# Own keys for the first two units, merged maxima tiles in the first chunk, and a new order of work

## The reference

```
h  = LN(x)
p  = h @ W_state.T + b_state ;  g = sigmoid(h @ W_gate.T + b_gate)
s_t = tanh(p_t + s_{t-1})                 # 1024 steps, one after the other
x1 = x + LN(g * s)
u  = LN(x1)
q, k, v = heads of rms(u) @ wq.T, wk.T, wv.T   (16 heads of 16; q, k are normed)
u += (softmax(causal(q k' / 4)) v) @ wo.T      (first 64 columns left as they are)
xf = rms(u) ; top 2 of 4 experts by softmax(xf @ gate_w.T)
u += sum of weights * expert(xf)               (all four experts are computed)
out = x1 + LN(u)
```

## Time and profile before

| | |
|---|---|
| median of 3 runs | 1585.27 us (1581.87 to 1589.87) |
| profiled execution | 1589.69 us |
| its span, first to last instruction | 1588.0 us |
| busy PE / DVE / ACT / POOL | 1403.0 / 1098.6 / 952.3 / 319.2 us |
| granted TensorE clock, mean | 0.933 |

### The profile page before, as it was taken

How to read it: one execution, slowest core, us unless ns; L and a number is a source line. 1 busy time by engine, 2 the same in 40 slices (tenths; PEclk the granted TensorE clock), 3 DMA queues, 4 the chain that set the end, 5 groups by cost and what they waited for, 6 DMA issues and landing times. The chain is left out here.

```text
span 1588.0 us, 33694 instructions
## 1 busy us (share of the span) xinstructions
PE 1403.0 (88%) x12320; PEld 1108.8 (70%) x12320; DVE 1098.6 (69%) x2916; ACT 952.3 (60%) x2092; POOL 319.2 (20%) x1146
## 2 busy tenths in 40 slices
PE   6915679999979799998998999999999999999997
PEld 3404567889867568688885577876686667857697
DVE  7776577553886975858888569786788777773342
ACT  2535465675556777775555673538546676468941
POOL 3343333223333323232332110001000010000000
PEclk9956578999998999899998899999999999999999
DMA  5585336754675545546656455665656657556343
GB/s 170 147 285 151 112 103 195 217 152 142 181 227 184 184 138 169 184 125 201 204 177 191 150 161 168 223 193 153 205 178 207 202 170 216 180 189 202 123 144 112
DMA packets 244276, 278.54 MB, mean 175 GB/s; under 512 B 37136, under 2 KB 167696, under 8 KB 243856
## 3 DMA queue, kind: packets, MB, share of 16 engines
q1 hardware_dynamic: 244112, 276.39, 56.6%
HBM read 234.18 MB, written 43.45 MB: 175 GB/s over the span
## 5 line engine op out<-in xcount | busy, mean ns | idle before, releaser
L1702 POOL TENSOR_TENSOR AD<-PX 128x8 f32<-128x8 f32 x1023 | 250.4, 245 | 553.3 <-ACT PX L928 537.3
L928 ACT ACTIVATE PX<-AD 128x8 f32<-128x8 f32 x1023 | 219.3, 214 | 232.0 <-POOL AD L1702 229.8
L996 ACT ACTIVATE work<-PS 128x1024 f32<-128x1024 f32 (+1 forms) x312 | 288.7, 960 | 79.5 <-PE PS L1042 77.8
L1501 DVE TENSOR_REDUCE mx<-PS 128x2 f32<-128x1024 f32 (+3 forms) x256 | 256.7, 1020 | 81.0 <-PE PS L1042 79.9
L1042 PE MATMUL PS<-work,vlx 128*32 128x256 f32 (+2 forms) x2816 | 240.6, 381 | 18.3 <-ACT work L996 7.5
L1042 PE MATMUL PS<-EP,u_e_l 128*128 128x256 f32 x1024 | 199.4, 289 | 6.9 <-DVE EP L1367 4.5
L1709 POOL TENSOR_SCALAR_AFFINE_SELECT work<-work 128x512 f32<-128x512 f32 x96 | 63.8, 674 | 638.1 <-ACT work L996 637.9
L1042 PE MATMUL PS<-WB,work 128*128 128x192 f32 x1024 | 181.2, 330 | 3.6 <-ACT work L1021 1.3
L1021 ACT ACTIVATE work<-PS 128x512 f32<-128x512 f32 x176 | 104.2, 596 | 132.7 <-PE PS L1042 131.2
L1042 PE MATMUL PS<-EP,WB 128*128 128x256 f32 x640 | 182.3, 285 | 0.0
L1042 PE MATMUL PS<-KT,QT 64*128 64x512 f32 (+3 forms) x768 | 151.9, 434 | 27.8 <-DVE mx L1501 12.9
(11 more groups left out here) (170 smaller groups left out, 2345.8 us busy)
## 6 DMA issues: line engine op xcount, KB each, us to landing
KT<-ktd SPq DMA_DIRECT2D x112, 512.0 KB, 4.8
WB<-wlo_e_l SPq DMA_DIRECT2D x160, 256.0 KB, 3.0
WB<-wlo_e_up SPq DMA_DIRECT2D x64, 256.0 KB, 3.0
ktd<-KTs SPq DMA_DIRECT2D x128, 128.0 KB, 2.2
WB<-wlo_e_w SPq DMA_DIRECT2D x64, 256.0 KB, 2.9
WB<-wdn_e_down SPq DMA_DIRECT2D x64, 192.0 KB, 2.7
KT<-ktd SPq DMA_DIRECT2D x48, 256.0 KB, 3.5
KT<-ktd SPq DMA_DIRECT2D x32, 384.0 KB, 4.1
```

Source lines behind the costliest of these rows:

```text
L928: eng.activation(cur, AD[n % 2], ACT.Tanh).then_inc(of(*key), 1)
L996: eng.activation(pt[:, :, :, q0:L], two("sc", *a).rearrange("p a (l q) -> p a l q", l=2)[:, :, :, q0:L], ACT.Exp).then_inc(of(*key), 1)
L1501: eng.tensor_reduce(o, two("mxm", *a)[:, :, 0:w], AX, ALU.max, negate=True).then_inc(of(*key), 1)
L1702: eng.tensor_tensor(AD[n % 2], PX[c % 2][:, :, :, t], PX[(n - 1) // L % 2][:, :, :, (n - 1) % L], ALU.add).then_inc(of(*key), 1)
```

## The change

Three edits.

1. Units 0 and 1 (`u < 2`) no longer use `KTs`. Their key tiles s = 0, 1 are copied to the two tiles of one `EP` pair (`own_keys`), and `mxm` and `sc` read them there. `ktm` and `kts` are not issued for these units. `kst` stays, with its source changed. The pair is held until the unit's last score (`sc`, group 3) and both stores are done.
2. In chunk 0 (`u < B`, four units) a maxima tile takes both planes of a group: 8 tiles in a unit instead of 16, each with twice the columns, and `mxr` reduces four rows of maxima at once.
3. New numbers in `STAY`, `START` and `AT`, thus another order on each engine.

```diff
-STAY = {"pe": 18.5, "act": 7.0}
+STAY = {"pe": 24.2, "act": 5.7}
-START = (114.6, 163.8, 192.7, 269.5, 332.7, 421.8, 507.9, 597.9, 743.8, ...)
+START = (101.2, 162.6, 177.3, 239.6, 336.5, 416.5, 521.4, 595.3, 735.9, ...)
 (all 27 rows of AT are new too)

 def tiles_of(u):
+            if u < B:
+                tiles.append((j, s, planes, 0, n))
+            else:
+                tiles += [(j, s, (pl,), k0, min(512, n - k0)) for pl in planes for k0 in range(0, n, 512)]

 arrange:
-  kt: take={"P2": (("kc", u, s),), "KTs": (("kst", u, s),)}
+  kt: take={"P2": (("kc", u, s),), **({"KTs": (("kst", u, s),)} if u >= 2 else
+        {"EP": (("sc", u, 3, 0), ("kst", u, 0), ("kst", u, 1))} if s == 0 else {})}
+            if u >= 2:
                 add("sp", ("ktm", u, j), ...)
-            for h in range((nkb + 3) // 4):
+            for h in range((nkb + 3) // 4) if u >= 2 else ():
                 add("sp", ("kts", u, g, h), ...)

+        def own_keys(u, s):
+            return EP[place[("kt", u, 0), "EP"]][s].rearrange("p k t -> p (k t)").rearrange("p (a k) -> p a k", a=8)

 mxm:
+                    if u < 2:
+                        kt = own_keys(u, s)[:, 2 * g:2 * g + 2, :]
+                        pe.wait_ge(*latest([("kc", u, 0), ("kc", u, 1)]))
+                    for x, pl in enumerate(pls):
+                        for par in range(2):
+                            ins = mm(ps[:, par, w * x:w * x + w], ..., x == 0, True, True)

 mxr:
+                    if len(pls) == 2:
+                        o = mx[:, s, :].rearrange("p (a h) -> p a h", a=2)[:, :, h:h + 2]
+                        x = two("mxm", *a)[:, :, 0:2 * w].rearrange("p a (l k) -> p a l k", l=2)
```

More of the change, by code:

```diff
@@ new lines @@
+STAY = {"pe": 24.2, "act": 5.7}
+START = (101.2, 162.6, 177.3, 239.6, 336.5, 416.5, 521.4, 595.3, 735.9, 806.3, 936.0, 1005.2, 1113.3, 1190.3, 1307.3, 1390.6)
+AT = {"piece": (-133.2, 84.2, 12.4, 109.4),
+      "post": (105.4, 80.1, -59.9, -28.2),
+      "prep": (-63.5, -85.9, -72.0, -5.3),
+      "value": (-196.8, 20.6, -143.0, -140.6),
+      "key": (-99.0, -64.8, 33.5, -55.6),
+      "query": (-40.6, -49.2, -91.2, -34.5),
+      "max": (-51.3, -43.8, -48.4, -39.2),
+      "maxima": (15.6, 0.5, 10.4, 44.6),
+      "bound": (71.1, -14.0, 109.5, 111.6),
+      "score": (37.1, 42.8, 43.2, 49.8),
+      "scores": (20.9, 11.4, 14.7, 16.6),
+      "av": (23.2, -22.9, 0.9, 17.7),
+      "merge": (22.7, -32.9, -7.9, 4.8),
+      "out": (-224.8, -29.1, -112.8, -84.9),
+      "gate": (-85.6, -244.9, -66.5, 50.2),
+      "l1": (7.3, 231.4, 238.0, 215.2),
+      "e0up": (189.4, 158.2, 57.5, 322.4),
+      "l2": (210.2, 275.6, 218.4, 193.1),
+      "e0dn": (371.7, 297.1, 375.7, -49.8),
+      "e1": (295.9, 250.0, 345.8, 230.4),
+      "l3": (220.9, 302.9, 201.9, 305.6),
+      "e3dn": (165.8, 332.2, 223.1, 268.9),
+      "e1dn": (272.2, 315.1, 325.6, 359.6),
+      "l4": (209.0, 255.5, 79.8, 276.9),
+      "e3up": (321.2, 310.5, 300.0, 298.5),
+      "e3out": (190.8, 294.9, 331.7, 465.0),
+      "fin": (230.3, 202.3, 202.0, 472.2)}
@@ L353, in arrange @@
             add("dve", ("kh", u, s), 2.33, d, ("qrs", u), ("cqk", 0), ("consts",), take={"QKP": (("kt", u, s),)})
[L354 removed]
+            add("pe", ("kt", u, s), 0.645, d, ("kh", u, s), mode="128", lat=DRAIN,
+                take={"P2": (("kc", u, s),), **({"KTs": (("kst", u, s),)} if u >= 2 else {"EP": (("sc", u, 3, 0), ("kst", u, 0), ("kst", u, 1))} if s == 0 else {})})
             add("act", ("kc", u, s), act(1024), d, ("kt", u, s))
@@ L366, in arrange @@
             dj = d + at["maxima"] * j / len(jobs)
-            add("sp", ("ktm", u, j), 0.35, dj - 5, *keys, *([("ktm", *prior["ktm"])] if "ktm" in prior else []), lat=4.5, take={"KT": (("mxm", u, ends[j]),)})
-            prior["ktm"] = (u, j)
-            for i, (j_, s, pl, k0, w) in enumerate(tiles):
+            if u >= 2:
+                add("sp", ("ktm", u, j), 0.35, dj - 5, *keys, *([("ktm", *prior["ktm"])] if "ktm" in prior else []), lat=4.5, take={"KT": (("mxm", u, ends[j]),)})
+                prior["ktm"] = (u, j)
+            for i, (j_, s, pls, k0, w) in enumerate(tiles):
                 if j_ != j:
@@ L1130, in _ @@
                     u, i = a
-                    j, s, pl, k0, w = tiles_of(u)[i]
+                    j, s, pls, k0, w = tiles_of(u)[i]
                     g, planes = jobs_of(u)[j]
-                    kt, n = KT[place[("ktm", u, j), "KT"]], 128 * key_blocks(u)
-                    kt = keys_of(kt[:, 512 * s:], 2, n) if u < B else keys_of(kt, len(planes), n)
+                    n = 128 * key_blocks(u)
+                    if u < 2:
+                        kt = own_keys(u, s)[:, 2 * g:2 * g + 2, :]
+                        pe.wait_ge(*latest([("kc", u, 0), ("kc", u, 1)]))
+                    else:
+                        kt = KT[place[("ktm", u, j), "KT"]]
+                        kt = keys_of(kt[:, 512 * s:], 2, n) if u < B else keys_of(kt, len(planes), n)
+                        pe.wait_ge(*done("ktm", u, j))
@@ L1144, in _ @@
-                    if diag < w:
+                    for x, pl in enumerate(pls):
+                        for par in range(2):
+                            rows = slice(64 * par, 64 * par + 64)
+                            ins = mm(ps[:, par, w * x:w * x + w], qt[rows, 2 * g + pl, 128 * s:128 * s + 128],
+                                     kt[rows, pl - planes[0], k0:k0 + w], x == 0, True, True)
+                    for x in range(len(pls)) if diag < w else ():
                         for i in range(2):
```

42 lines of the change are left out of this document (22 added, 20 removed).

## The result

The changed kernel takes 1593.51 us (median of 18 runs, 1588.54 to 1598.75), the kernel before 1585.48 (18 runs, 1576.40 to 1591.12). The ratio is 1.0052, 95% interval 1.0037 to 1.0068: slower by 8.2 us (5.9 to 10.8). Forecast were 1575 us and "faster", with an outer range of 1558 to 1594 and a chance of 0.16 for slower. So the time lies just inside the range, and the direction is wrong. So the two traces differ by 1.1 us where the medians differ by 8.0. They can show what moved; the price has to come from timed runs.

The account below looks back on a forecast made before the run. TensorE bounds it from 280 us, with holes before 280 and after 402. Experts 19 us earlier: 7 + 3, plus 1 + 2, is 13; less 3 given back, 10 off 1585.27 makes 1575 us (1567 to 1583; outer 1558 to 1594).

Parts of the forecast that it names:

- Edits, first part: Units 0 and 1, own keys: maxima start 4.7, their pass 6, scores 8; unit 0's experts 19 us earlier, near 211.
- named marks of success: Unit 0's maxima before 150, output projection before 200, first expert before 215; TensorE work over 40 from 160 to 230.
- Edits, second part: Merged maxima tiles, units 0 to 3: 4.9 us less VectorE work, 1 us added to the gain.
- What the earlier experts are worth: Before 280: 19 us at 0.80 instead of 0.44 give 7 us, unit 1's experts 3; 10 together.
- what is given back at the gate: After 402: step 511 stays, so experts done before are missing; 0 to 10 us given back, taken as 3.
- The new order: Newly searched order on all engines: taken as 2 us gained, with -10 to +12 as ends.
- The third rival: Recurrence late beside earlier experts: gate 6 us later, 10 missed, 4 for order, against 10 won; 1595, chance 0.17.
- the sum's own gain: Before 280: 10 us from earlier experts, 1 from merged maxima and 2 from the order, 13 us.
- The first rival: Work pulled out of 402 to 557 is missed there one for one: 3 us less, 1582, chance 0.22.
- the named signs of failure: First expert after 225, unit 0's second layer waiting, gate after 408, or 402 to 600 losing what the first stretch won.
- The rule of the Trainium skill: VectorE and GpSimd share a port lock: reductions from PSUM cost the recurrence nothing, experts' subtractions hold it up; no term changed.

Follow-up runs that it names:

- k3: Kernel before, every engine's order kept, with both edits (own keys and merged maxima tiles): 0.9996 (0.9968 to 1.0023) of before, median 1587.62 us.
- k9: Changed kernel with 45 recurrence steps between 204 and 508 left out, order otherwise kept, output not the reference's: 1.0053 of the kernel before.
- k13: Both edits; order of the kernel before up to 640 us, the changed kernel's behind it: 1.0027 of before, 1591.21 us.
- k14: Both edits; the changed kernel's order up to 640 us, that of the kernel before behind it: 1.0132 of before, 1608.25 us.
- the kernels of the table: Both edits in all; orders of the kernel before and the changed kernel, whole or crossed at 640 or 150 us: 0.9996 to 1.0132 of before.
- k11: Both edits with due times from a new search that replays orders with disturbed durations: 1.0065 of before, median 1598.05 us.
- k12: Both edits with due times from a second result of that disturbed-duration search, from another start: 1.0081 of before, median 1598.28 us.
- k5: Changed kernel with six exponentials of units 0 and 1 moved 1 to 8 recurrence steps later on ScalarE: 1.0056 of the kernel before.
- k7: Changed kernel with 100 ScalarE instructions between 160 and 416 us placed up to 40 tanhs later: 1.0096 of the kernel before.
- k4: Kernel before with 76 small extra GpSimd adds ahead of recurrence steps, 55 between steps 200 and 254: 1.0027 of before.
- k6: Kernel before with two extra GpSimd adds before each of steps 203 to 254, one before every tenth from 261 to 501: 1.0080 of before.

## Why the prediction was wrong

**Edits, first part: right in kind, mis-sized.** The 32 loads of 128 KB are gone. Maxima started 2.8 us earlier (4.7 forecast), their pass became 5.7 shorter (6), the scores 4.2 (8). That makes 12.7 of the 18.7 us in these terms. The scores fell short because I counted 2.4 us from score to score as if only loads stood between them; in TensorE's new order unit 1's maxima do. A further 3.9 were lost between them: the maxima's copy and the way from the fourth score to the output projection, which I had counted as fixed, took 5.3 us more, and what follows 1.4 less. Unit 0's experts came 8.8 us earlier instead of 19, and TensorE did 34.3 us from 160 to 230 where "over 40" was named. The named marks of success were missed as well: maxima at 150.31 instead of before 150, the output projection at 204.59 instead of before 200. The held `EP` pair cost nothing, as taken: unit 1's last score stands at 201.53, 20 us before unit 0's first expert matmul.

**Edits, second part: right.** The reductions are 686 and 1220 ns. VectorE is only 1.7 us less busy in all, against the 4.9 that I worked out from count times mean. The busy column of the forms gives 33.3 before and 29.7 after, 3.6 less; the rest lies in its other instructions.

**What the earlier experts are worth.** The forecast priced them at 10 us, 11 with the merged tiles, and 8 net of what is given back at the gate. With the order kept they came 3.6 us earlier (k3), and nothing came out of that which can be measured: 0.9996, between 5.1 us less and 3.6 more. So this term was too large as well: 8 us for the edits is outside the interval.

**The new order: the step that failed.** I took it as 2 us gained, with -10 to +12 as ends, and the gate as staying at 402 with 3 us given back. Both were wrong. With the edits alone the time is that of before (0.9996, k3), with the new order it is 1.0052: the order costs 8.9 us instead of winning 2. It does 5.8 us more work in the first hole, 28 less in the second, and 13 more from 600 to 1000. Its gate is 14.6 us late. The forecast priced a step at 0.69 or 0.90 us and asked who is beside it. It overlooked what stands ahead of it in the same queue: the exponentials that wait for unit 0's scores make 9 of the 10 us by which step 255 is later. And it took VectorE to be ready for the gate, where the new order has other steps first.

The third rival had the direction and nearly the time, 1595, but by luck as to its terms. It put 6 us on the gate, 10 on missed work and 4 on a misfitted order, by another cause: steps beside experts, not behind exponentials. It also set these 20 against 10 us, where the sum's own gain was 13; with 13 it comes to 1592. Measured are 14.6 us at gate 4, of which 4 taken back brought nothing that can be seen (k9), and an order whose start costs 4 to 22 us depending on what follows (k13, k14). The first rival's mechanism, work missed after 402, is seen as well. Two of the named signs of failure came out: the gate after 408, and more lost after 402 than was won before.

**What stays open.** Why the plan ranks the kernels of the table, k14 aside, the other way round than the chip does: from 1608.9 to 1595.7 us it promises 13 us, and the chip takes 9 more. (Against the plan of the kernel before itself, 1598.9, it promised only 3.2.) k11 and k12, found by a harder search, promise 6 and 4 us more and are no faster. That fits a search that finds orders in which the plan's own errors pay, but no run here shows that cause; a plan with durations from the traces was not tried. Nor is it settled which instructions between 150 and 640 us carry the start's cost. One candidate is untested: step 255, and with it the gates of units 2 and 3, stayed 8 us or more late in the changed kernel, k9, k11, k12 and k14. k5 and k7 had step 255 earlier (196.1 and 190.6) and were no faster, but even there the gate of unit 2 came only at 196.5 and 196.8, against 199.69 in the changed kernel and 189.23 before.

**The rule of the Trainium skill** (SBUF — State Buffer, section "SBUF: two separate sides"). In the changed kernel the recurrence's adds that ran wholly beside a reduction from PSUM took 0.20 to 0.21 us. The 12 that began during a subtraction of 128x1024 on line 1388 took a mean of 1.05, at most 1.25, and each ended 0.05 to 0.07 us after the subtraction. The trace agrees with the rule on both, and the longer reductions cost the recurrence nothing, as said.

## What to carry to other kernels

Where every engine runs a fixed order, a chain of tiny steps also waits for whatever the big instruction ahead of it in its own queue waits for; look at that, before pricing the chain by its mean step. Filling a hole from work that would have filled the next one is no gain: add up the work of both stretches. And test an edit in the order kept, then the new order by itself; a searched order is a change of its own, and a planned gain of 0.2 to 0.8% was no evidence here.

## What was not expected of the hardware

An extra add costs the recurrence less than its own duration. In k4 a step with nothing else in its way takes 0.67 us instead of 0.52, 0.14 more, though the extra add is recorded with 0.19: the next add starts 0.14 us after it and overlaps its end. With two extra adds (k6) a step takes 0.81.

```profile
180.41 0.19 POOL L1707 TENSOR_TENSOR spare<-PX 128x1 bf16<-128x1 f32 x1 [0.33 <-ACT PX L932]
180.55 0.20 POOL L1709 TENSOR_TENSOR AD<-PX 128x8 f32<-128x8 f32 x1
```

Fifty-five such adds would be 7.8 us, but step 255 moved by only 3.9 (192.85 against 188.91). My reading is that the rest is hidden in steps that stand behind an exponential or a copy anyway.

And the granted clock is lower where work is missing: in 402 to 557 it is 0.92 in the kernel before and 0.80 to 0.82 in every kernel with the new start. The matmuls that are left take longer there: 115.37 us of busy time for 945 of them, 0.122 each, against 132.40 for 1138, 0.116 each.
